# The low weights of heads 4 and 5 formed on GpSimd, in an SSD attention and ternary FFN kernel on one core

## The reference, cut to what matters

```
zxbcdt = u @ W_in.T                      # z 1024, x 1024, B 64, C 64, dt 8
dt = softplus(zxbcdt[..., -8:] + dt_bias)
xBC = silu(causal_conv4(xBC) + conv_b)
y = ssd(x, dt, -exp(A_log), B, C, D)     # 8 heads of 128, state 64
yg = y * silu(z)
yn = yg * rsqrt(mean(yg**2) + eps) * norm_w
x1 = layernorm(u + yn @ W_out.T)
out = layernorm(x1 + ffn(x1))            # ternary weights, hidden 2048
```

## Time and profile before

| | |
|---|---|
| median of 3 runs | 1354.16 us (1352.62 to 1354.37) |
| profiled execution, its own time | 1353.24 us |
| span of its trace | 1351.1 us |
| PE busy | 1329.7 us (98%) |
| DVE busy | 1042.9 us (77%) |
| ACT busy | 785.2 us (58%) |
| POOL busy | 666.9 us (49%) |
| granted PE clock | 0.999 |

### The profile page before, as it was taken

One profiled execution on the slowest core, in us unless ns is written; L12 is line 12 of the kernel. 1 busy time (PEld: TensorE's weight loads), 2 busy tenths in 40 slices (PEclk: granted clock), 3 DMA queues, 4 the chain that ended last, 5 costly groups with the idle time before them and its releaser, 6 DMA issues.

```text
span 1351.1 us, 24906 instructions
## 1 busy us (share of the span) xinstructions
PE 1329.7 (98%) x9318; PEld 865.9 (64%) x9318; DVE 1042.9 (77%) x1855; ACT 785.2 (58%) x1561; POOL 666.9 (49%) x640
## 2 busy tenths in 40 slices
PE   8999999999999999999999999999999999999998
PEld 5555565665656556556567677777777777777774
DVE  7987877878868878688786987777777767777675
ACT  6895783865847838568385545454454545454441
POOL 3793472764846737445357434344343435344331
PEclk9999999999999999999999999999999999999999
DMA  7564453353643634324564423222231322221001
GB/s 251 180 197 162 126 149 94 93 144 102 157 108 81 180 89 114 127 94 146 156 150 171 121 87 75 67 52 83 59 79 42 72 71 64 70 59 52 32 32 63
DMA packets 162776, 143.64 MB, mean 106 GB/s; under 512 B 101344, under 2 KB 123232, under 8 KB 161504
## 3 DMA queue, kind: packets, MB, share of 16 engines
q1 hardware_dynamic: 162656, 142.05, 37.1%
HBM read 99.93 MB, written 27.39 MB: 94 GB/s over the span
## 4 chain that ended last, share of the span: by engine, by line
PE 79%; DVE 4%; issue 4%; POOL 2%; ACT 1%; DMA 0%; POOLq 0%; DVEq 0%; ACTq 0%
PE ring L942 19%; PE ring L1158 15%; PE ring L971 9%; PE p_turn L1138 8%; PE p_y L1138 7%; PE p_st L1138 6%; PE p_seg L1138 6%; PE p_y L1016 3%; PE p_y L1024 2%; PE p_st L1006 2%; PE p_turn L996 1%; PE ring L1195 1%; POOL sq_sum L1658 1%; POOL raw L1650 0%; PE p_turn L987 0%
## 5 line engine op out<-in xcount | busy, mean ns | idle before, releaser
L942 PE MATMUL ring<-u_split,weights 128*128 128x512 f16 x1620 | 372.0, 379 | 0.5 <-DVE x_ch L1849 0.5
L1754 POOL TENSOR_TENSOR xdt<-xdt 128x512 f32<-128x512 f32 x64 | 100.8, 1575 | 327.0 <-DVE xdt L2246 327.0
L942 PEld LDWEIGHTS ring<-u_split,weights 128*128 128x128 f16 x1620 | 154.0, 98 | 167.8 <-issue 2.7
L971 PE MATMUL ring<-w_out,raw 128*128 128x512 f16 x672 | 147.7, 379 | 1.0 <-DVE c_ch L1876 1.0
L1844 DVE SCALAR_TENSOR_TENSOR acc<-ring,taps,acc 128x511 f32<-128x511 f32 (+2 forms) x192 | 143.8, 749 | 4.5
L971 PEld LDWEIGHTS ring<-w_out,raw 128*128 128x128 f16 x672 | 65.3, 99 | 79.6 <-DVE c_ch L1876 3.4
L1650 POOL TENSOR_TENSOR raw<-yg,raw 128x512 f16<-128x512 f32 x64 | 78.7, 1231 | 61.7 <-ACT raw L1397 61.3
L1366 ACT ACTIVATE xdt<-p_turn,dts 128x128 f32<-128x128 f32 x256 | 72.7, 375 | 53.3 <-PE p_turn L996 53.2
L1645 POOL TENSOR_TENSOR yg<-y_ch,z_ch 128x512 f32<-128x512 f32 x64 | 81.5, 1274 | 36.7 <-DVE y_ch L1979 36.7
L1375 ACT ACTIVATE p_seg<-cum_rows,cum 128x128 f32<-128x128 f32 x256 | 80.9, 390 | 5.2 <-DVE seg L1957 5.2
L1658 POOL TENSOR_TENSOR sq_sum<-sq_sum,sq 128x512 f32<-128x512 f32 x56 | 71.6, 1279 | 0.0
(11 more groups left out here) (400 smaller groups left out, 3262.1 us busy)
## 6 DMA issues: line engine op xcount, KB each, us to landing
cum_rows<-cum_dram SPq DMA_DIRECT2D x64, 256.0 KB, 4.1
quant<-in_w_ffn SPq DMA_DIRECT2D x24, 512.0 KB, 4.6
quant<-in_w_ffn SPq DMA_DIRECT2D x48, 256.0 KB, 4.9
cum_g<-cum_dram SPq DMA_DIRECT2D x64, 128.0 KB, 4.6
rows<-in_u_tok SPq DMA_DIRECT2D x32, 256.0 KB, 5.5
x_dram<-rows SPq DMA_DIRECT2D x32, 256.0 KB, 2.1
tern_ug<-quant SPq DMA_DIRECT2D x32, 256.0 KB, 3.1
u_raw<-in_u_t SPq DMA_DIRECT2D x7, 1024.0 KB, 8.1
```

What stands on the lines that cost most here:

```text
L942: mm = pe.matmul(bank_k[:, :], w_in[:, ws, k, col:col + P], us[:, par, k * T:(k + 1) * T], start=(i == 0), stop=(i == 3 * KD - 1))
L971: mm = pe.matmul(ring[b][:, :], ys[:, h, c * P:(c + 1) * P], w_out[:, ws, h, :], start=(h == 0 and ys is y_hi and ws == 0), stop=(h == H - ...
L1754: pool.tensor_tensor(tile_[:, 1, :, :], tile_[:, 0, :, :], tile_[:, 1, :, :], ALU.mult).then_inc(hid_ok, 1)
```

## The change

POOL forms the low weights of heads 4 and 5 too, each as its own pair of instructions. Head 4 stands ahead of `c_decay(0,0,1)`, head 5 between `wout_scale(0)` and head 7. The DVE instruction for both heads goes. `wout_low(0)` leaves its place behind head 7 and stands behind the gates and the `b_decay` of slot 2. The table `POOL_HEADS` sets which semaphore count PE waits for.

```
-POOL_HEADS = [2, 3, 7]
+POOL_HEADS = [2, 3, 4, 5, 7]

 def head_weights(h):
-    return 2 + h if h < 2 else 2 + h // 2
+    return 2 + h if h < 2 else 4
...
             w_lo_head(2)
             w_lo_head(3)
             b_decay(0, 0, 0, turn_use(0, "b0"))
+            w_lo_head(4)
             c_decay(0, 0, 1)
             b_decay(0, 0, 1, None)
             wout_scale(0)
+            w_lo_head(5)
             w_lo_head(7)
-            wout_low(0)
...
                     if not is_at(n, NB):
                         b_decay(n, par, p, turn_use(n - 1, "b") if p == 0 else None)
+                    if is_at(n, 0) and p == 2:
+                        wout_low(0)
                     if gate_slot(n, p):
                         for q in range(2):
                             y_low(n, p, q)
...
             dt_first(1, turn_use(0, "dt"))
             magnitude(1)
-            w_lo(4)
```

## The result

The changed kernel takes 1355.74 us in the median of 22 runs (1354.55 to 1358.77), the kernel before 1353.72 us (22 runs): ratio 1.0017, 95% interval [1.0012, 1.0023], which is 1.6 to 3.1 us slower; the two medians lie 2.0 us apart. The profiled execution took 1356.49 us (before 1353.24), its span is 1354.8 us.

A forecast was written before the change was run, and what follows sets the result against it. PE bounds the kernel, waiting on DVE directly and through ACT. Head 4: 0; DVE's 0.15 gain overtaken; late da: +2.1. That gives 1355.3 from the profile, 1356.3 from the median; middle 1355.8, range 1353.0 to 1358.0.

The forecast's parts named there:

- one chain: POOL's work delays DVE's small products, wout_low(0) holds da, and PE's cum_proj waits for da: +2.1 us, chance 0.52.
- Head 4 free: POOL's pair for head 4 ends at 34.2, 1.0 us before c_decay can go at 35.23: cost 0.
- At most 0.15 us of DVE's 2.28 usable: Without its instruction DVE waits for ACT at cb_conv and within; at most 0.15 us reaches da.
- `dt_w` held until 53.6: dt_w arrives 0.14 us behind the start of POOL's head 7 subtraction and waits for its end: DVE 1.1 us late.
- `wout_low(0)` ends at 63.0: POOL's four subtractions take 4.51 us from 58.5; dt_q waits for the last, so da starts 2.1 us late.
- Both orders of `dt_w` and POOL's subtraction end alike: If dt_w slips in ahead of POOL at 51.5, da is still 1.9 us late, through wout_low(0).
- Behind `cum_proj` everything keeps its distance: Later DVE and ACT work moves 2.1 us; PE's waits of 0.54 and 1.20 us keep their sizes.
- Rival 1: The small DVE products slip between POOL's: 1353.1 us, chance 0.18.
- rival 3: The freed DVE time reaches PE and removes its three idle times, 2.17 us: 1351.1 us, chance 0.08.
- Rival 2: POOL's two subtractions on weights take 3.85 us, not 2.13; da starts near 65.1: +3.6, 1356.8 us, chance 0.16.
- rival 4: Half the delay is absorbed behind 120 us, where DVE waits for loads: 1354.3 us, chance 0.06.
- `dt_s`, `dts` and `da` follow freely: After dt_q the other three small DVE products follow as before, 0.49 us from dt_q's end to da's start.

The follow-up runs named there:

- e1: The kernel before without DVE's instruction for the low weights of heads 4 and 5, which are zero here; ratio to before 1.0001.
- e2: The changed kernel with the four instructions of wout_low(0) cut to 8 of 512 columns each; ratio to before 0.9997.
- e5: The changed kernel with wout_low(0) back behind the low weights of head 7, ahead of the gates; ratio to before 1.0011.
- e10: The changed kernel with POOL starting wout_low(0) only when DVE has written da; ratio to before 1.0022.
- e3: The changed kernel with DVE's dt_w, dt_m and dt_r moved ahead of the convolution of B and C; ratio to before 1.0011.
- e7: The kernel before with head 4's low weights on POOL in its wait for grow and head 5's alone on DVE; ratio to before 1.0005.
- g1: The e7 kernel with head 6's low weights also early on DVE, right behind head 5's; ratio to before 1.0002.
- e4: The changed kernel with dt_w, dt_m and dt_r early and wout_low(0) cut to 8 of 512 columns each; ratio to before 0.9998.

## Why the prediction was right

The forecast was +2.1 us by one chain, 1355.8, and the median is 1355.74. The chain is right and +2.1 is met by A and B (+2.07 and +2.06) and by the medians (+2.0). That the total agrees within 0.06 us is luck: 1355.8 is the middle between two start values 0.9 us apart, and the interval of the difference alone is 1.5 us wide. The profile answers step by step; 1.69 us of the start is to be added to each forecast time.

- Head 4 free, ready at 34.2: measured 33.49 + 2.14 = 35.6 with POOL's `b_decay` 1.46 us later than before, and still 1.3 us ahead of `c_decay`.
- At most 0.15 us of DVE's 2.28 usable: `cb_conv` waits 1.41 us for ACT, and e1 gives 0.13 in B.
- `dt_w` held until 53.6, DVE 1.1 to 1.2 us late: 2.05 us for `dt_w`, 1.28 us in e2. The ground given was a row with two SBUF inputs; what carried over to `dt_w` was the row of `dt_m`, which has one. The prediction also left out that this delay reaches PE before `da` does, by 0.73 us at the tile at 58.23; that wait lies inside the 2.1 us and adds nothing.
- `wout_low(0)` ends at 63.0, `da` starts at 63.6, `cum_proj` at 63.9: 64.70, 65.24 and 65.58, against 64.7, 65.3 and 65.6.
- Both orders of `dt_w` and POOL's subtraction end alike: not shown for the changed kernel itself, where `dt_w` came second. In e5 it was first and A is the same, but there the gates and `b_decay` held the products in place of `wout_low`. In e10 it was first too, but `wout_low` was held back there, and A fell to 15.74.
- Behind `cum_proj` everything keeps its distance: waits of 0.55 and 1.21 us, and ACT's `gated` at 68.18 (forecast 66.5 + 1.69 = 68.2). PE's first tile of W_out starts at 138.70 instead of 134.90, 3.80 later, which is 1.69 + 2.1. The load of W_out had more room than forecast: issued at 64.72 and landed 5.1 us later (7.1 before), at 69.8, it was 2.5 us ahead of `wout_scale(1)` at 72.35, not 0.6. Its row among the DMA issues of the changed kernel:

```profile
rows<-in_w_out SPq DMA_DIRECT2D x1, 1024.0 KB, 5.1
```

Rival 1 (short products slip between POOL's) is refuted by e3, rival 3 (freed DVE time reaches PE) by e1. Rival 2 did not come about: both subtractions took 2.13 and 2.14 us. Of rival 4 there is a trace only: PE is 3.76 us behind the kernel before at `cum_proj` and 3.30 at 165 us, because a wait for ACT of 0.67 us at 162.34 was 0.18 at 165.64. Over the experiments this wait lies between 0.17 and 0.75 without any relation to A, so I take it for scatter. One step was worded too loosely: that `dt_s`, `dts` and `da` follow freely holds only because `wout_low` was in its last instruction when `dt_q` came.

No version that I ran beats the kernel before. The three waits of PE, 2.17 us together, hang on DVE and ACT behind 52 us, and no edit took them away without a new wait.

## What to carry to other kernels

Before work goes from DVE to POOL, list what DVE does in the stretch that POOL now fills. Beside POOL's two-input instructions of this kernel, a DVE instruction with two SBUF inputs, and here a TENSOR_SCALAR with one, took what was left of POOL's instruction, however short it was itself; a chain of four short ones took one POOL instruction for each link. Put POOL's work beside DVE instructions that read PSUM, or into a wait of POOL's own in which DVE has no such instruction (e7 shows the second for head 4; the first was not tried). And time freed on an engine is worth only what its next wait leaves of it.

## What the runs showed that I had not expected

- DVE and POOL took turns instruction by instruction, in e3 and in g1. Two DVE instructions next to each other (4.28 us) cost 2.0 us more than one of the same length (2.28 us), since POOL's subtraction came in between.
- POOL's scaling, with one tensor input, held DVE far less. The small `dt_n`, which reads SBUF only, took 0.19 us in the middle of it in the kernel before (scaling from 43.71 to 46.48) and 0.51 in g1; over all the kernels it lies between 0.19 and 0.61. A small product that came 0.1 to 0.2 us behind the start of a scaling, near 18.2 us, took 0.9 to 1.0.

```profile
44.90 0.19 DVE L1897 SCALAR_TENSOR_TENSOR dt_n<-dt_x 128x32 f32<-128x32 f32 x1
```

In g1:

```profile
45.45 0.51 DVE L1898 SCALAR_TENSOR_TENSOR dt_n<-dt_x 128x32 f32<-128x32 f32 x1
```

- The granted clock of TensorE fell to its lower level (0.50) for one tile in four of the ten profiled executions (changed kernel, e4 and e10 near 20 us, e3 near 65 us), and that tile of 12 matmuls then took 4.28 to 4.45 us instead of 2.75. In one profiled execution that is almost as large as the effect under study; counting from a fixed instruction behind it, just ahead of the change, removes it. Where the fall comes inside the stretch that is counted, as in e3, only the granted clock of the stretch tells it from the edit.
